# Two 16-head attentions of a four-stage kernel: row maxima of two heads in one VectorE operation over two PSUM banks

## The reference

```python
x = x + _L0_attn_ref(_layernorm(x), ...)   # A: 16 heads of 8, rotary, biases, full softmax over 1024 keys
x = x + _L0_ffn_ref(_layernorm(x), ...)    # B: six layers of local attention and gated feed-forward
x = x + _L1_attn_ref(_layernorm(x), ...)   # C: 16 heads of 8, rotary, causal softmax
x = x + _L1_ffn_ref(_layernorm(x), ...)    # D: small attention and a mixture of experts
```

```python
scores = jnp.einsum('bhqd,bhkd->bhqk', q, k) / jnp.sqrt(jnp.float32(hd))
attn = jax.nn.softmax(scores, axis=-1)
out = jnp.einsum('bhqk,bhkd->bhqd', attn, v)
```

## Time and profile before

| | us |
|---|---|
| median of 3 runs (lowest, highest) | 5104.03 (5103.71, 5106.9) |
| the profiled execution, its own time | 5100.34 |
| span of the profiled execution | 5099.0 |
| PE, DVE, ACT, POOL busy | 4696.4, 4381.7, 3299.9, 2893.1 |
| stage A, first to last row maximum | 46.5 to 783 |
| stage C, first to last row maximum | 3913 to 4484 |

### The profile page before, as it was taken

One profiled execution on the slowest core, in us unless ns is written; L12 is line 12 of the kernel. 1 busy time (PEld: TensorE's weight loads), 2 busy tenths in 40 slices (PEclk: granted clock), 3 DMA queues, 4 the chain that ended last, 5 costly groups with the idle time before them and its releaser, 6 DMA issues.

```text
span 5099.0 us, 145718 instructions
## 1 busy us (share of the span) xinstructions
PE 4696.4 (92%) x60680; PEld 3199.9 (63%) x60680; DVE 4381.7 (86%) x9187; ACT 3299.9 (65%) x6490; POOL 2893.1 (57%) x3053
## 2 busy tenths in 40 slices
PE   6999997999999999999999999999996999989978
PEld 3333334677777777777777777777774555545567
DVE  8999997899989998999899989999995777768666
ACT  4888885566666666666666666666663676756632
POOL 1330303778877887787778877877772222006644
PEclk7999998999999999999999999999996999979989
DMA  0000100000000000000000000000000000000000
GB/s 24 1 1 1 33 5 24 27 11 12 13 27 10 12 13 27 10 12 13 27 10 12 13 27 11 12 15 10 8 4 26 2 2 2 2 16 1 1 1 17
DMA packets 51748, 63.46 MB, mean 12 GB/s; under 512 B 12820, under 2 KB 41258, under 8 KB 50322
## 3 DMA queue, kind: packets, MB, share of 16 engines
q1 hardware_dynamic: 51090, 54.14, 3.6%
HBM read 25.17 MB, written 4.19 MB: 6 GB/s over the span
## 4 chain that ended last, share of the span: by engine, by line
PE 59%; DVE 23%; issue 6%; ACT 6%; POOL 3%; DMA 2%; SPq 0%; DVEq 0%; POOLq 0%; ACTq 0%
PE psum L558 7%; PE psum L1163 7%; PE psum L1240 6%; PE psum L1225 6%; PE psum L529 6%; PE psum L1208 4%; DVE a_top L714 4%; PE psum L1172 4%; PE psum L1280 2%; DVE b_cross L1483 2%; DVE x L1479 2%; PE psum L545 2%; PE psum L1290 2%; PE psum L526 2%; DVE x L1515 1%
## 5 line engine op out<-in xcount | busy, mean ns | idle before, releaser
L1631 POOL TENSOR_TENSOR x<-x,b_cross 128x512 f32<-128x512 f32 x768 | 990.4, 1300 | 123.4 <-DVE b_cross L1483 123.4
L1637 POOL TENSOR_TENSOR x<-x,b_norm 128x512 f32<-128x512 f32 x768 | 793.4, 1044 | 277.6 <-ACT b_norm L1319 277.2
L1240 PE MATMUL psum<-b_w_vo,b_mixed 128*128 128x128 f32 x6144 | 748.9, 275 | 0.2 <-issue 0.2
L1240 PEld LDWEIGHTS psum<-b_w_vo,b_mixed 128*128 128x128 f32 x6144 | 724.0, 192 | 10.6 <-issue 0.3
L714 DVE TENSOR_REDUCE a_top<-psum 128x1 f32<-128x512 f32 x1024 | 643.5, 683 | 59.7 <-PE psum L529 55.7
L1312 ACT ACTIVATE b_square<-psum 128x512 f32<-128x512 f32 x768 | 465.7, 606 | 338.3 <-PE psum L1163 315.6
L641 ACT ACTIVATE a_prob<-psum 128x512 f32<-128x512 f32 x1024 | 558.3, 604 | 103.0 <-PE psum L545 95.2
L1479 DVE TENSOR_TENSOR x<-psum,b_table 128x512 f32<-128x512 f32 x768 | 519.3, 676 | 12.6 <-ACT b_square L1312 11.2
L1483 DVE TENSOR_TENSOR b_cross<-psum,b_table 128x512 f32<-128x512 f32 x768 | 521.3, 679 | 0.0
L1361 ACT COPY b_mixed<-psum 128x512 f32<-128x512 f32 x768 | 417.4, 601 | 147.1 <-PE psum L1225 147.1
L1491 DVE TENSOR_REDUCE b_bounded<-b_square 128x8 f32<-128x512 f32 x768 | 500.9, 672 | 12.1 <-ACT b_square L1312 8.4
(11 more groups left out here) (354 smaller groups left out, 10663.1 us busy)
## 6 DMA issues: line engine op xcount, KB each, us to landing
b_prev<-b_xs_x SPq DMA_DIRECT2D x24, 384.0 KB, 3.5
ab<-in_L_ffn_Wqkv SPq DMA_DIRECT2D x6, 1024.0 KB, 7.0
b_shifted_x<-y SPq DMA_DIRECT2D x24, 224.0 KB, 2.6
b_shifted_f<-y SPq DMA_DIRECT2D x48, 112.0 KB, 2.1
ab<-in_L_ffn_Wqkv SPq DMA_DIRECT2D x6, 512.0 KB, 7.4
ab<-in_L_ffn_Wo SPq DMA_DIRECT2D x6, 512.0 KB, 9.1
b_prev<-b_xs_x SPq DMA_DIRECT2D x24, 112.0 KB, 3.5
x<-in_L_attn_x SPq DMA_DIRECT2D x4, 512.0 KB, 7.0
```

The source lines that it names most:

```text
L1240: made = e.matmul(banks[n][:, 0:D], mixed[:, h, :], w_vo[l % 2][:, h, :], start=h == 0, stop=h == 2 * PAIRS - 1)
L1631: e.tensor_tensor(turned, turned, crossing[:, :, ::-1, :], ALU.add).then_inc(sem["roped"], 1)
L1637: e.tensor_tensor(rh, rh, bcast(norm[i % 2][:, 1, HPC * c:HPC * (c + 1)], 2, LDIM), ALU.mult).then_inc(sem["scaled"], 1)
```

## The change

- First products are steps of two heads. The pair writes two neighbouring banks, (0, 1) or (2, 3), and signals once; DVE reduces both banks in one operation over `chip.psum[:, n:n + 2, 0:wide]` to two columns of `top2`.
- The rings of banks are dealt anew. Steps whose bank DVE empties (`first`, `weights`, `turn_back`, `conclude`) share the two pairs (0, 1) and (2, 3), and each takes a whole pair. Steps whose bank ACT empties (`second`, `turn_x`, `project`, `turn_k`, `turn_q1`, `turn_q2`, `turn_o`) share banks 4, 5 and 6.
- In C the mask matmuls of the two heads of a pair of first products alternate: for each of the four the one head, then the other, and then both products. Those of the second products stay as they are.
- The first `shift` piece waits for the last two first steps, not three.

```diff
+def paired(causal):
+
+    return True
+
+
 def mha_order(causal, widths):
...
             for n, (t, c, h) in enumerate(pairs[part]):
-                for head in range(2 * h, 2 * h + 2):
+                for head in ((2 * h,) if paired(causal) else (2 * h, 2 * h + 1)):
                     put(base + n, "first", i, t, c, head)
...
-    singles = cycle((3, 4, 5, 6))
-    number, slot = chip.place(order, dict(
-        first=cycle((0, 1, 2)), **{kind: singles for kind in ("second", "weights", "turn_x", "project", "turn_k", "turn_q1",
-                                                           "turn_q2", "turn_back", "turn_o", "conclude")}))
+    twins = paired(causal)
+    heads_at_once = 2 if twins else 1
+    to_scalar = ("second", "turn_x", "project", "turn_k", "turn_q1", "turn_q2", "turn_o")
+    to_vector = ("first", "weights", "turn_back", "conclude")
+    if twins:
+        maxima, singles = cycle((0, 2)), cycle((4, 5, 6))
+        rings = {**{kind: maxima for kind in to_vector}, **{kind: singles for kind in to_scalar}}
+    else:
+        singles = cycle((3, 4, 5, 6))
+        rings = {**{kind: singles for kind in to_scalar + to_vector}, "first": cycle((0, 1, 2))}
+    number, slot = chip.place(order, rings)
...
                     q.wait_ge(emptied[n], use - 1)
-                    part = slice(ROWS * head, ROWS * (head + 1))
                     if corner:
                         q.wait_ge(sem["blocks_cast"], 1)
-                        for m in range(4):
-                            e.matmul(banks[n][:, wide - P + ROWS * m:wide], blocks[part, 0, m, :],
+                    for m in range(4 if corner else 0):
+                        for twin in range(heads_at_once):
+                            part = slice(ROWS * (head + twin), ROWS * (head + twin + 1))
+                            e.matmul(banks[n + twin][:, wide - P + ROWS * m:wide], blocks[part, 0, m, :],
                                      blocks[part, 1, m, ROWS * m:P], start=m == 0, stop=False,
-                                     skip_group_check=True, tile_position=(ROWS * head, 0))
-                    e.matmul(banks[n][:, 0:wide], q1[i % 2][part, P * t:P * (t + 1)], kt[i % 3][part, BANK * c:hi],
-                             start=not corner, stop=True, skip_group_check=corner,
-                             tile_position=(ROWS * head, 0)).then_inc(filled[n], 1)
+                                     skip_group_check=True, tile_position=(part.start, 0))
+                    for twin in range(heads_at_once):
+                        part = slice(ROWS * (head + twin), ROWS * (head + twin + 1))
+                        made = e.matmul(banks[n + twin][:, 0:wide], q1[i % 2][part, P * t:P * (t + 1)],
+                                        kt[i % 3][part, BANK * c:hi], start=not corner, stop=True,
+                                        skip_group_check=corner, tile_position=(part.start, 0))
+                    made.then_inc(filled[n], 1)
...
-                    e.tensor_reduce(top2[i % 2][:, t, c, head:head + 1], banks[n][:, 0:wide], AX.X,
-                                    ALU.max).then_inc(emptied[n], 1)
+                    e.tensor_reduce(top2[i % 2][:, t, c, head:head + heads_at_once],
+                                    chip.psum[:, n:n + heads_at_once, 0:wide], AX.X, ALU.max).then_inc(emptied[n], 1)
...
-                        for back in range(3):
+                        for back in range(2 if twins else 3):
```

## The result

The changed kernel takes 5156.09 us (median of 4 runs, 5141.75 to 5161.61) against 5105.47 (4 runs, 5103.71 to 5111.39): ratio 1.0093, 95% interval 1.0071 to 1.0115. Its profiled execution took 5161.61, 61.3 us more than the profiled one of before.

The account below looks back on a forecast made before the run. Stage A was taken as bound by a loop through PE, DVE and three banks, replaced by one as long over ACT. A's +50 and C's +8 made 58 us, forecast 5157; own range 5125 to 5190, widened to 5100 to 5192.

Parts of the forecast that it names:

- The loop, 2.69 for plain periods: Stage A: second product, exponential, hand-back, next product and drain, values product take 2.69 us; a plain period gains 0.02.
- A step in ACT's ring, +0.53: Stage A: a transpose or projection takes one of three banks, so its period lengthens by 0.53 us; 57 such, +30.
- `turn_back`, 3.24: Stage A: it takes a pair, so the next first products wait; period 3.24 us against 2.71; 27 periods, +15.
- the term for `shift`: Stage A: `shift` operations, said to stretch a period to 2.88 us, leave the path; 16 x -0.17 = -3 us.
- the opening, before the first values product: Start of stage A: 22 slots of first products alone each gain 0.07 us, -2 in all.
- The sum of A: Stage A: all counted terms together make it 50 us slower; +25 or +75 if copies cost less or more.
- Three against four banks: Second products' ring: three banks stand between two uses instead of four, so a period's last second product waits for the first's.
- C, +8: Stage C: late periods against earlier ones give +0.5 us a unit, +8 in all, between -15 and +25.
- The mask term: Stage C: alternating masks let the second head's product come up to 0.08 us sooner; at most 20 us, 3 counted.
- The rival of the costlier ring: Stages A and C: ACT's backlog or late products idle DVE too, +30 and +15: 5200 us; chance 0.07.
- DVE as the bound: Stage A: DVE bounds and exponentials keep up, plain periods fall to about 2.5 us: total 5040; chance 0.15.
- The cancelling case: Stages A and C: ring steps half hidden, plain periods 2.63 us, C at -15: total 5100 to 5110; chance 0.08.

## Why the prediction held, point by point

**The loop, 2.69 for plain periods: right.** It is 2.65, over ACT as foreseen: 0.57 + 0.59 + 0.06 + 0.43 + 1.00. The gain over 2.71 is 0.06, three times the 0.02 counted.

**A step in ACT's ring, +0.53; `turn_back`, 3.24: mechanism right, sum too large.** One such step costs one interval of ACT, which is now 0.49, and the period is 3.14 instead of 3.22; two make 3.61 instead of 3.71; `turn_back` came to 3.25. Besides, I let all these periods start from 2.71. The ones of before had a mean of 2.86 (`turn_k`) and 3.17 (`project`), so the difference of the means is 0.29 and 0.21, not 0.51. And the term for `shift` was a misreading: the period of 2.88 is the one behind a `turn_back`. By the last column of the table the periods give +37, and the opening, before the first values product, gave 4 back (foreseen 2). The sum of A was +50 and is +32: the terms that failed are the lengths, up to 0.10 too long, and the periods taken for free that were not.

**Three against four banks: shown.** Three banks alone gave 3.16 in the periods with another step, and 49 us in A.

**C, +8: about right for the periods, but the opening had no term.** From the first values product on C is +9.1, where +8 was foreseen. The opening is -15.1, where the sum has nothing; together -6. The fourth bank brings the opening: with three banks and single reductions it took 59.4, with four 45.2. Its clock was 0.50 before and 0.61 after, so how much of the 15 us is the bank's own is not separated. And -6 is not much more than C varies by itself: the same code for C took 569.8 when A was left alone, and the kernel before took 570.4 and 572.8. The period of the earlier trace rows went from 2.41 to 2.73 (+0.32, foreseen +0.5) and that of the earlier trace rows from 3.14 to 2.98 (-0.16, foreseen -0.09), from these rows after:

```profile
4188.53 0.64 PE L574 MATMUL psum<-c_prob,c_v 128*32 128x256 f32 x8
...
4191.26 0.42 PE L574 MATMUL psum<-c_prob,c_v 128*32 128x128 f32 x8
...
4199.53 1.06 PE L574 MATMUL psum<-c_prob,c_v 128*32 128x512 f32 x8
...
4202.51 1.06 PE L574 MATMUL psum<-c_prob,c_v 128*32 128x512 f32 x8
```

The mask term was mis-sized: 3 of at most 20 counted, some 37 measured, and the price of the pairs in C with it. Without alternation the working has C at +11; measured against the kernel before it was +30 and +48. The two errors cancel in the +8, which is luck.

**What no term held: the ends, +33.** I costed nothing behind the last first product, where the ring of three is all that PE has and two pairs stand idle. The rival of the costlier ring said that short waits could lower PE's clock, by 22 us at most in A's steady part. (A mean clock lower by 0.06 is 12% more of the time at half speed, not 6%, so that bound should have been 44.) There the clock stayed as it was, at 1.00 from the first values product to the last maximum but for a few us at the start; it fell in the ends.

**The total** of 5157 against 5156.09 is thus partly luck: in the profiled executions, A 18 too high and C 14 too high against 33 of the ends left out, with 1.7 for the rest, lead from 58 to 61. The 5157 is also not quite the sum, which gives 5158 on the profiled execution and 5162 on the median of before. By the medians the change cost 51 us.

**The rivals.** DVE as the bound is ruled out: giving it 0.13 us more in a period (two operations for one) left plain periods at 2.65. The cancelling case is ruled out by the run with three banks, and plain periods at 2.65, not 2.63. The Trainium skill (TensorE: Matmul & The Clock Gate, section on PSUM-queue cycling) tells of clock lost where PE idles briefly between groups. The trace agrees for A's end, where waits of 0.65 went before the fall (0.77 in the mean); it does not for A's steady part, where PE waits 0.42 in the plain periods and keeps 1.00. The Trainium skill (VectorE: DVE Perf Modes, section on the TRN2 errata) gives a PSUM operation of DVE 120 cycles beside its columns, and an estimate from it is that a pair saves 125 ns; back to back the runs show (2.48 - 2.35) / 2 = 65.

**The profile foreseen.** DVE busy in A: foreseen 640 of 786, came 649 of 768. Waits of PE for ACT appeared and those for maxima shrank; pair reductions of 1.22 and 1.13, foreseen 1.21 and 1.13.

## What stays open

Why the masks' order moves the clock of C is not settled: with pairs, two executions of each order agree, but no run isolates which gap in PE's work decides, and the kernel before keeps 0.91 with its masks head by head. Nor is it shown what makes the clock fall 15 us before C's last maximum, or how much of C's shorter opening is clock. The size of C in the kernel with three banks (616.1) has the same low clock and the same open cause. Stretches were not tried in which PE waits for a set time.

## What to carry to other kernels

When banks are moved from one ring to another, price the loop from a bank's use to its next use on both rings, and count for each extra step in the ring one interval of the engine that empties it. But subtract only from periods that are free today: take the mean by kind of period, not the tidy median one. And cost the stretches where only one of the rings works: here C's start gained 15 us by the fourth bank of first products and the two ends lost 33 by the third bank of the others. Five banks instead of three at the ends gave 34 us back in the profiled executions, 28 by the medians, by one line of dealing.

## What was new about the hardware

One DVE reduction over two PSUM banks shows no price for the crossing: 1220 ns for 1024 columns, where the lengths at 128 and 512 columns make 1215. And the clock follows small things: with pairs in C, the same matmuls in another order of eight masks had 0.84 to 0.87 instead of 0.93, and C was 36 to 54 us of 564 longer, 13 of these at most without the clock. Waits of 0.65 in periods of 2.6 us without first products went before the fall to 1.2 GHz, while the waits of 0.42 in the plain periods of 2.65 with them did not; which part of that difference decides is not shown.
